# Two-layer perceiver on one core: helical attention with squares over two PSUM banks and one logarithm for both sums

## What is computed

```
q = x @ Wq.T + bq ; k = x @ Wk.T + bk ; v = x @ Wv.T + bv          # 16 heads of 8 features
q_hel = einsum('bshd,hed->bshe', qh, Whel) + bhel                  # 64 features per head; k_hel alike
qn = l2norm(q_hel over its 32 pairs of two) ; kn alike             # x / sqrt(x0*x0 + x1*x1), per pair
qn, kn = scramble(...)                                             # swaps token and pair member, reshapes
helical = einsum('bhpsc,bhptc->bhst', qn, kn) / 32
dot = einsum('bshd,bthd->bhst', qh, kh) / sqrt(8)
attn = softmax(0.5 * dot + 0.5 * helical)
out = (attn @ v) @ Wo.T + bo
```

## Time and profile before

| | us |
|---|---|
| median of 3 runs | 539.52 |
| lowest, highest run | 536.23, 542.24 |
| profiled execution, device time | 540.14 |
| its span from first to last instruction | 538.4 |
| outside the span | 1.74 |

### The profile page before, as it was taken

The page is one execution under the profiler, slowest core; times in us unless marked ns, Lnnn a source line. Parts: engine busy times, 40 slices in busy tenths (PEclk is TensorE's granted clock), DMA queues, the critical chain, the costliest instruction groups (busy, mean ns, idle before and its releaser), DMA issues.

```text
span 538.4 us, 9067 instructions
## 1 busy us (share of the span) xinstructions
PE 469.3 (87%) x2963; PEld 333.6 (62%) x2963; DVE 416.4 (77%) x1013; ACT 309.8 (58%) x581; POOL 117.1 (22%) x114
## 2 busy tenths in 40 slices
PE   5785888999999999786788978998868899999996
PEld 2342455777777777452435667887855457777774
DVE  4479958767777776779886888989987758888885
ACT  4245125567766675441233589989642247777774
POOL 2002002122221220073000253345300022222320
PEclk9979799999999999997899889999897969999999
DMA  8962000111101100000010000000001011111101
GB/s 308 409 194 62 0 2 0 60 58 59 26 34 58 58 1 1 0 2 0 1 41 1 1 2 2 1 1 2 3 0 41 0 39 39 40 39 39 39 2 39
DMA packets 9118, 22.97 MB, mean 43 GB/s; under 512 B 2244, under 2 KB 4468, under 8 KB 9080
## 3 DMA queue, kind: packets, MB, share of 16 engines
q1 hardware_dynamic: 9080, 22.49, 11.9%
HBM read 21.96 MB, written 0.52 MB: 42 GB/s over the span
## 4 chain that ended last, share of the span: by engine, by line
PE 58%; DVE 23%; ACT 8%; issue 5%; DMA 3%; SPq 2%; DVEq 0%; ACTq 0%
PE pair L364 12%; PE pair L366 12%; PE pair L365 12%; DMA arena<-in_zT 3%; PE pair L737 2%; PE pair L758 2%; PE turn L540 2%; PE pair L763 1%; DVE Y L1328 1%; PE pair L439 1%; DVE st L1305 1%; PE turn L358 1%; PE turn L364 1%; DVE arena L1669 1%; ACT YT L879 1%
## 5 line engine op out<-in xcount | busy, mean ns | idle before, releaser
L364 PE MATMUL pair<-yTh,wh 128*128 128x512 f32 x134 | 62.6, 467 | 3.3 <-ACT work L965 3.3
L1768 DVE TENSOR_TENSOR pair<-work,turn 128x512 f32<-128x512 f32 x64 | 44.5, 696 | 17.5 <-ACT work L1134 16.1
L1134 ACT ACTIVATE work<-pair,vec 128x512 f32<-128x512 f32 x64 | 44.0, 689 | 24.0 <-PE pair L366 18.7
L1191 POOL TENSOR_TENSOR wl<-wraw,wh 128x512 fp32r<-128x512 f32 x24 | 31.1, 1300 | 113.5 <-ACT wh L901 113.5
L366 PE MATMUL pair<-yTh,wl 128*128 128x512 f32 x134 | 53.4, 398 | 0.0
L365 PE MATMUL pair<-yTl,wh 128*128 128x512 f32 x134 | 53.4, 398 | 0.0
L1545 DVE TENSOR_TENSOR pair<-work,pair 128x512 f32<-128x512 f32 x48 | 33.3, 695 | 24.0 <-PE pair L366 20.6
L439 PE MATMUL pair<-g3b,zerob 128*128 128x512 bf16 x178 | 47.5, 410 | 0.7 <-DVE Y2b L1625 0.7
L965 ACT ACTIVATE work<-pair 128x512 f32<-128x512 f32 x64 | 38.3, 598 | 14.6 <-PE pair L366 13.7
L989 ACT ACTIVATE ph<-pair 128x512 fp32r<-128x512 f32 x48 | 28.8, 599 | 24.2 <-DVE pair L1545 24.2
L364 PE MATMUL pair<-ph,wh 128*128 128x512 f32 x96 | 38.8, 404 | 2.7 <-DVE pl L1565 2.6
(11 more groups left out here) (292 smaller groups left out, 1184.5 us busy)
## 6 DMA issues: line engine op xcount, KB each, us to landing
wraw<-in_w SPq DMA_DIRECT2D x8, 768.0 KB, 4.3
arena<-in_zT SPq DMA_DIRECT2D x8, 514.0 KB, 10.7
arena<-in_z SPq DMA_DIRECT2D x8, 512.0 KB, 11.4
wraw<-in_w SPq DMA_DIRECT2D x7, 512.0 KB, 3.2
mat<-in_mat SPq DMA_DIRECT2D x1, 768.0 KB, 14.9
mat<-in_mat SPq DMA_DIRECT2D x48, 2.0 KB
row<-in_row SPq DMA_DIRECT2D x1, 576.0 KB, 14.7
mat<-in_mat SPq DMA_DIRECT2D x1, 520.0 KB, 15.1
```

What stands on the lines that cost most here:

```text
L364: pe.matmul(out, ah, bh, start=start, stop=False)
L1134: act.activation(act_out[q % 2], UP1[q % 4], ACT.Relu, bias=vec[:, bass.ds(at, 1)])\
L1191: pool.tensor_tensor(wl[k][:, cols], wraw[:, cols], wh[k][:, cols].bitcast(F32), ALU.subtract)\
L1768: dve.tensor_tensor(UP1[q % 4], act_out[q % 2], bank[h], ALU.mult).then_inc(m["mul"], 1)
```

## The change

`squares(m)` issues one Square of 128x1024 over both banks of `pair[m % 2]`, once both blocks of the operand have landed, and raises `h_sq` once. POOL's wait is counted anew for that. `n2(2u)` and `n2(2u+1)` lie side by side in the work area, so `inverse(2u)` takes one Ln of 128x1024 over both, once POOL has added both sums, and waits for it; each operand keeps its own Exp. `inverse(2u+1)` then holds its Exp alone, behind its wait.

```
             def squares(m):
                 if m >= 2:
                     act.wait_ge(h_n2, m - 1)
-                for j in range(2):
-                    n = 2 * m + j
-                    act.wait_ge(h_hel, n + 1)
-                    act.activation(sq(m)[:, j * HN:(j + 1) * HN], bank[2 + n % 4], ACT.Square).then_inc(h_sq, 1)
+                act.wait_ge(h_hel, 2 * m + 2)
+                act.activation(sq(m), pair[m % 2].rearrange("p j x -> p (j x)"), ACT.Square).then_inc(h_sq, 1)
 
             def inverse(m):
 
-                act.wait_ge(h_n2, m + 1)
-                step(act.activation(n2(m), n2(m), ACT.Ln, scale=float(2 ** 20), bias=lntiny[:, :]))
+                if m % 2 == 0:
+                    act.wait_ge(h_n2, m + 2)
+                    both = slot(8, 2)
+                    step(act.activation(both, both, ACT.Ln, scale=float(2 ** 20), bias=lntiny[:, :]))
                 act.activation(n2(m), n2(m), ACT.Exp, scale=-0.5, bias=(cq, ck)[m % 2][:, :]).then_inc(h_inv, 1)
...
             def add_squares(m):
-                pool.wait_ge(h_sq, 2 * m + 2)
+                pool.wait_ge(h_sq, m + 1)
```

## The result

| | before | after |
|---|---|---|
| median of 20 runs, us | 538.21 | 540.38 |
| lowest, highest run | 532.16, 542.24 | 537.10, 542.41 |
| profiled execution: device time, span | 540.14, 538.4 | 540.86, 539.1 |

A forecast was written before the change was run, and what follows sets the result against it. PE was taken to lead in the middle units, ACT only from key(2) to keys(3). Unit 0's +1.7 us less 0.43 us in units 1 and 2, 0 elsewhere, gave +1.3 us: 540.8 us, range 537.5 to 543.5.

The forecast's parts named there:

- Prices: On ACT, a wide Square costs 1.032 us and a wide Ln 1.140, saving 0.12 and 0.31 us a unit.
- Unit 0: The Ln waits for POOL's second sum; DVE's normalise starts 1.83 us later and the chain is 1.7 us later.
- ACT's stretch: Units 1 and 2, chain mostly on ACT: logarithms of unit 1 (0.31) and squares of unit 2 (0.12) gain 0.43 us.
- Units 3 to 5: Middle units: the wait for PE takes in the squares' saving, the logarithms' lies behind key; gain 0.
- One sign: Units 3 to 5: ACT's idle time before extract, 0.53 us a unit, was to become longer.
- The clock: PE's low clock around rotate of unit 1, after a gap grown from 3.10 to 4.9 us: delay 1.7, or 1.3 to 3.4.
- the clock that comes back at the same moment: Case in unit 0: PE gets through less work at the low level, so the delay is about 1.3 us.
- No change that can be told: Whole kernel: +1.3 us lies under the 1% (5.4 us) that three runs can tell; within 1% given 0.90.
- ACT as the bound of all units: Rival: ACT's saving of 3.4 us counts in all units, -1.7 us in sum, 537.8 us; chance 0.10.
- a wait in every unit: Rival: every unit waits for POOL's second sum as unit 0 does, 13.6 us, 553 us; chance 0.05.
- the cost of the bank edge: Rival: wide operations cost what two narrow ones did, or more, 541.2 to 541.7 us; chance 0.70 together with the forecast.
- The rival of the clock: Rival: the clock stays low once more after unit 0, 1.7 us more, +3.0 in sum, 542.5 us; chance 0.15.

The follow-up runs named there:

- the Ln alone: The kernel before with only the wide Ln of the change, Squares and POOL's wait as before: ratio to before 1.0032, over all runs 1.0024.
- unit 0 apart: The change, but with one Ln for each sum in unit 0, units 1 to 7 merged: ratio to before 1.0014, over all runs 1.0003.
- unit 0 as before: The change, but with Squares and logarithms of unit 0 in their old form: ratio to before 1.0031, over all runs 1.0014.
- POOL's sums first: The change, but in unit 0 POOL adds both sums before it does stack_q(1): ratio to before 1.0030, over all runs 1.0005.
- the extra Squares: The kernel before with one or two more unused Squares of 128x512 on ACT in units 3 and 4: single runs, 534.32 and 538.88 us.
- Squares alone: The change without its inverse: wide Squares and POOL's new count, logarithms as before; ratio to before 0.9984, over all runs 0.9997.
- the second profile of the change: The same changed kernel run again in a second set of 12 runs: ratio to before 1.0050, over all runs 1.0042.
- the four filled kernels: Matmuls of zeros in PE's gap before unit 1's rotate, added to the change, before, unit 0 as before, POOL's sums first: all-runs ratios 1.0061, 1.0006, 1.0034, 1.0065.

## Why the prediction was right

*Prices.* 1.032 and 1.140 us were forecast from the slope between 4 and 512 columns; 1.025 and 1.149 were measured. In unit 2, on the path, the two wide Squares took 1.93 us (forecast 1.94).

*Unit 0.* The Ln at 312.53 was 312.39, DVE at 314.45 was 314.33, PE at 315.33 was 315.23 with the gap of 4.91 us (all 0.1 sooner, as the stage began 0.11 sooner). The step is confirmed by the edits that take it back in part or whole, and by the Ln alone, which brings it all. One step beside it was off: ACT's first Square of unit 1 came 1.6 us later and not 1.1, as it waited 0.57 us for PE's blocks; PE's scores came 1.9 us later, so it cost nothing.

*ACT's stretch.* 0.43 us was forecast, 0.46 measured (12.27 to 11.81 us), and 11.81 or 11.82 in the kernels with unit 0 apart, unit 0 as before and POOL's sums first. The parts are confirmed alone: the Squares took 12.27 to 12.15 (0.12, as forecast), the Ln to 11.93 (0.34 for 0.31).

*Units 3 to 5.* Zero: 10.98 us between `dots` in both, and the extra Squares show the room of 0.6 us. One sign came out the other way. I had said that ACT's idle time before `extract` would grow; in unit 4 it shrank from 0.53 to 0.39 us, because the second wide Square waits for PE's second block and both together take 2.18 us where the four narrow ones took 2.06. The time saved shows one step earlier instead, as ACT's wait before `query`, 0.62 us for 0.28.

*The clock.* This is the term that was mis-sized. I took 1.7 us of delay with 1.3 and 3.4 as its ends; in the first profile the delay at `key(2)` was 1.26 us, in the second 2.43, and with the Ln alone 2.63. The first is the prediction's case of the clock that comes back at the same moment (at 318.9, before at 318.5), priced at 1.3. In the second the low stretch was twice as long, and that cost 1.17 us more and not the 1.7 of the prediction. The long stretch, to which the prediction gave 15 in 100, was in two of the three profiles with a gap of 4.9 to 5.0 us ahead of an unfilled `rotate(1)`, and in none of the seven with an unfilled gap of 3.1 to 3.9 us; ten profiles are few, and the same length came after a wait of 2.6 us in unit 7, so that the gap causes it is not shown. With the shorter outcome `keys(3)` is 0.80 us late, with the longer 1.97; the forecast of 1.3 lies between.

*The whole.* Measured +2.2 us of medians (+2.3 of the means), against +1.3, so the forecast change was 0.9 us too small. That 540.8 came within 0.4 us of 540.38 is partly luck: the base of 539.52 came from three runs and was 1.3 us above the median of 20, and the two errors nearly cancel. "No change that can be told" went by the scatter of three runs; with 20 of each, 0.4% can be told.

At `keys(3)` the two profiles of the change are 0.8 and 2.0 us late, at the end of the stage 1.3 and 2.8. The runs' records bear on this too: over all 91 runs of before that list a clock, the mean granted clock of the execution was 0.9509, over 32 of the change 0.9442. The means of these runs differ by 2.1 us (540.4 and 538.3). Within the runs of before 0.01 of clock goes with 3.2 us and within those of the change with 1.6 us, so 1.1 to 2.2 us of the 2.1 go with the clock. This is a correlation, and part of the lower clock may come from the longer gap itself. Where the profiles lose a lead after `keys(3)` can be seen. The scores of unit 6 ran at the low clock, 3.4 to 3.7 us for 2.0, with all of unit 0 as before, with unit 0 apart, with Squares alone, with Ln alone, with two extra Squares, in the second profile of the change and in three of the four filled kernels (in the fourth, sums first, they took 2.4 us). In the first profiles of before and of the change, with POOL's sums first and with one extra Square they did not. What decides in which execution the clock is low there stays open. No edit was tried on PE's waits for DVE in units 6 and 7.

*The rivals.* ACT as the bound of all units is refuted by the extra Squares; a wait in every unit by leaving unit 0 apart; the cost of the bank edge by the durations. The rival of the clock came true in part of the profiles.

## What to carry to other kernels

Merging two operations saves little when the engine overlaps its instructions already, and it turns two waits into one for the later of both: look at the first round of the pipeline, where no older work fills the wait, and price it there. Before counting an engine's saving, put extra work on it in one unit and see how much of it vanishes; here it was 0.6 us for each 11 us. A longer gap on TensorE can have a second price that varies from run to run, and filling one gap didn't help here when the next engine's queue opened another behind it.

## What the runs showed of the hardware

TensorE's granted clock came in low stretches of 3.4 us or 6.8 us within the first 30 us of the stage, nothing between in these 14 profiles (two filled kernels had none), and after a gap of 4.9 us it took either. In the two profiles of the change the clock fell 0.3 us after the matmul that ended the gap (315.5 for 315.23) and 1.0 us before it (310.9 for 311.83): the same gap, and the fall is not tied to the first matmul. Equal waits of 2.6 us in unit 7 were followed by scores at the high clock in one kernel and at the low in another. A ScalarE read of 128x1024 float32 over two PSUM banks took 1.025 us, 0.417 more than one of 512 columns, as many as 512 more columns cost by the slope of before (0.424), so the edge between banks added nothing that shows. DVE's normalisation of Y took 4.06 us in the change with the gap filled, in place of 3.08 us. POOL's operations ran beside it for 3.8 us there (two sums and `stack_q`) and for 2.6 us in the change (one sum, `stack_q` and 0.1 us of the next); whether that made it longer was not tried.
